# A decoder layer stack on one core: ScalarE's order in the second block of a batch, and queries transposed ahead of keys

## The reference, cut to what matters

```python
for i in range(DEPTH):                       # DEPTH = 6
    x = attn_layer(shift_tokens(x), Wqkv[i], q_scale[i], k_scale[i], Wo[i]) + x
    x = ffn_layer(shift_tokens(x), ln_g[i], ln_b[i], W1[i], b1[i], W2[i], b2[i]) + x

def attn_layer(x, Wqkv, qs, ksc, Wo):        # 16 heads of 64
    q, k, v = split(x @ Wqkv)                # per head
    q = l2norm(q) * qs; k = l2norm(k) * ksc  # then rotary tables on q and k
    out = local_attention(q, k, v)           # windows of 32, each sees itself and the one before
    return out @ Wo

def ffn_layer(x, g, bln, W1, b1, W2, b2):
    xn = (x - mu) / sqrt(var + 1e-05) * g + bln
    a, gate = split(xn @ W1 + b1, 2)
    return a * gelu(gate, exact) @ W2 + b2
```

## Time and profile before

| what | value |
|---|---|
| timed runs | 2187.67, 2188.90, 2188.56 us; median 2188.56 us |
| profiled execution, its own time | 2173.51 us |
| its span | 2171.7 us |
| PE busy | 2003.2 us, 92% |
| DVE busy | 1411.9 us, 65% |
| ACT busy | 1397.0 us, 64% |
| POOL busy | 1085.8 us, 50% |
| mean granted TensorE clock | 0.983 of full |
| chain that ended last | PE 70%, ACT 10%, issue 10%, DVE 9% |

### The profile page before, as it was taken

One profiled execution on the slowest core, in us unless ns is written; L12 is line 12 of the kernel. 1 busy time (PEld: TensorE's weight loads), 2 busy tenths in 40 slices (PEclk: granted clock), 3 DMA queues, 4 the chain that ended last, 5 costly groups with the idle time before them and its releaser, 6 DMA issues.

```text
span 2171.7 us, 74796 instructions
## 1 busy us (share of the span) xinstructions
PE 2003.2 (92%) x32616; PEld 1186.4 (55%) x32616; DVE 1411.9 (65%) x1975; ACT 1397.0 (64%) x2029; POOL 1085.8 (50%) x709
## 2 busy tenths in 40 slices
PE   8999998788999999999999999999999999999997
PEld 5655655355555555555555555555555555555552
DVE  1454444676677776767677767776777676767662
ACT  5555554466677666766676666666766676667763
POOL 0000000586666666556666656665656665666550
PEclk9999998899999999999999999999999999999998
DMA  3000000122223222232222322222322223222220
GB/s 108 2 1 1 2 20 30 37 64 61 60 70 80 75 71 62 58 94 74 72 57 68 90 55 72 73 60 66 80 76 69 62 60 90 70 70 61 61 61 20
DMA packets 82066, 128.11 MB, mean 59 GB/s; under 512 B 17230, under 2 KB 28108, under 8 KB 81740
## 3 DMA queue, kind: packets, MB, share of 16 engines
q1 hardware_dynamic: 81740, 123.33, 21.7%
HBM read 21.55 MB, written 1.05 MB: 10 GB/s over the span
## 4 chain that ended last, share of the span: by engine, by line
PE 70%; ACT 10%; issue 10%; DVE 9%; DMA 0%; ACTq 0%; DVEq 0%; SPq 0%
PE ps L617 13%; PE ps L613 12%; PE ps L639 8%; PE ps L693 6%; PE ps L678 6%; PE ps L685 5%; PE ps L426 3%; PE ps L622 3%; PE ps L626 2%; ACT work L993 2%; PE ps L658 2%; DVE work L1249 2%; DVE SS L1141 2%; PE ps L519 1%; PE ps L440 1%
## 5 line engine op out<-in xcount | busy, mean ns | idle before, releaser
L1418 POOL TENSOR_TENSOR work<-work,RS 128x1024 f32<-128x1024 f32 x192 | 365.2, 1902 | 406.4 <-ACT RS L967 405.1
L1096 DVE TENSOR_TENSOR work<-ps,work 128x512 f32<-128x512 f32 (+1 forms) x288 | 249.1, 865 | 341.1 <-ACT work L1025 304.6
L617 PEld LDWEIGHTS ps<-ident,work 128*128 128x128 f32 x3072 | 344.5, 142 | 167.9 <-issue 120.2
L617 PE MATMUL ps<-ident,work 128*128 128x128 f32 x3072 | 395.3, 276 | 25.9 <-ACT work L993 21.9
L1429 POOL TENSOR_TENSOR work<-work 128x1024 f32<-128x1024 f32 x96 | 226.9, 2364 | 124.9 <-DVE work L1101 124.8
L1437 POOL TENSOR_TENSOR work<-work 128x1024 f32<-128x1024 f32 x96 | 225.9, 2353 | 100.2 <-DVE work L1101 100.2
L1101 DVE TENSOR_TENSOR work<-ps,work 128x512 f32<-128x512 f32 (+1 forms) x288 | 247.3, 859 | 0.0
L1037 ACT ACTIVATE work<-work 128x1024 f32<-128x1024 f32 x96 | 101.5, 1057 | 206.6 <-DVE work L1181 206.3
L1141 DVE TENSOR_REDUCE SS<-work 128x16 f32<-128x1024 f32 x192 | 232.1, 1209 | 0.0
L685 PEld LDWEIGHTS ps<-work 64*32 64x32 f32 x12288 | 134.4, 105 | 148.1 <-issue 132.6
L613 PE MATMUL ps<-WQ,XS 128*128 128x512 f32 x384 | 188.6, 614 | 8.0 <-issue 4.3
(11 more groups left out here) (184 smaller groups left out, 3208.9 us busy)
## 6 DMA issues: line engine op xcount, KB each, us to landing
work<-work SPq DMA_DIRECT2D x576, 128.0 KB
work<-work SPq DMA_DIRECT2D x336, 64.0 KB
WQ<-in_wqkv SPq DMA_DIRECT2D x6, 512.0 KB, 3.7
WK<-in_wqkv SPq DMA_DIRECT2D x6, 512.0 KB, 4.5
WV<-in_wqkv SPq DMA_DIRECT2D x6, 512.0 KB, 3.5
WO<-in_wo SPq DMA_DIRECT2D x6, 512.0 KB, 3.9
work<-ZR SPq DMA_DIRECT2D x48, 64.0 KB
W<-in_w SPq DMA_DIRECT2D x6, 341.0 KB, 3.1
```

What stands on the lines that cost most here:

```text
L617: m = nc.tensor.transpose(flat(R)[:, t * 128:t * 128 + 128], src[:, t * 128:t * 128 + 128], ident[:, :])
L1096: V.tensor_tensor(h16(cos_part[:, j, cols]), h16(src), rotary_tabs[:, at:at + 64].unsqueeze(1).broadcast_to([PARTS, heads_in, 64]), ALU.mu ...
L1418: U.tensor_tensor(h16(qk_norm[:, j, :]), h16(cos_part[:, j, :]), inv_norms[:, j, :].unsqueeze(2).broadcast_to([PARTS, 16, 64]), ALU.mult). ...
```

## The change

Three moves; no instruction is added or removed.

1. In every step PE transposes the queries ahead of the keys, and ScalarE copies the transposed queries ahead of the two key halves. In the second block's step the chunk 2 pieces of the feed-forward keep their places between and behind the two.
2. In the second block's step ScalarE's first Gelu stands ahead of the values' copy, directly behind the table load.
3. `invert_norms` of the keys, at the end of the first block's step, goes into the second block's step, behind the square of the queries and the heads' copy and ahead of the table load.

```diff
@@ TensorE, step @@
                 if b:
+                    if a:
+                        pe.wait_ge(q_sin, g + 1)
+                    pe.wait_ge(q_normed, g)
+                    turn(bank_z, qk_norm[:, 0, :]).then_inc(q_turned, 1)
+                if f is not None and n == 1:
+                    pe.wait_ge(gate_gelu, 3 * f + 2)
+                    hid_gate(2, bank_f)
+                if b:
                     pe.wait_ge(k_normed, g)
                     if d:
                         pe.wait_ge(heads_turned_copied, g - 2)
                     turn(bank_y, qk_norm[:, 1, :], 0, 4).then_inc(k_turned, 1)
                     turn(bank_y, qk_norm[:, 1, :], 4, 8).then_inc(k_turned, 1)
-                if f is not None and n == 1:
-                    pe.wait_ge(gate_gelu, 3 * f + 2)
-                    hid_gate(2, bank_f)
-                if b:
-                    if a:
-                        pe.wait_ge(q_sin, g + 1)
-                    pe.wait_ge(q_normed, g)
-                    turn(bank_z, qk_norm[:, 0, :]).then_inc(q_turned, 1)
@@ ScalarE, step @@
                 if f is not None and n == 1:
+                    if b:
+                        invert_norms(g - 1, 1)
                     nc.scalar.preload_act_table_set(GELU)
+                    gelu(f, 0, bank_f)
                 if b:
...
                     A(v_rows[:, (n - 1) % 2, :], flat(bank_x), ACT.Copy).then_inc(values_copied, 1)
-                if f is not None and n == 1:
-                    gelu(f, 0, bank_f)
...
                 if b:
+                    act.wait_ge(q_turned, g)
+                    A(q_t[:, :, :], turned(bank_z), ACT.Copy).then_inc(q_turned_copied, 1)
+                if f is not None and n == 1:
+                    gelu(f, 2, bank_f)
+                if b:
                     for half in range(2):
                         act.wait_ge(k_turned, 2 * g - 1 + half)
...
-                if f is not None and n == 1:
-                    gelu(f, 2, bank_f)
-                if b:
-                    act.wait_ge(q_turned, g)
-                    A(q_t[:, :, :], turned(bank_z), ACT.Copy).then_inc(q_turned_copied, 1)
...
-                if a:
+
+                if a and not (f is not None and n == 0):
                     invert_norms(g, 1)
```

## The result

| | before | after |
|---|---|---|
| timed runs, median | 2188.11 us (2182.88 to 2188.90, 4 runs) | 2166.66 us (2163.55 to 2167.32, 4 runs) |
| profiled execution, span | 2171.7 us | 2161.7 us |
| mean granted TensorE clock | 0.983 | 0.988 |

The ratio is 0.9907 with a 95% interval of 0.9887 to 0.9927: faster by 0.9%, where I had forecast 0.3% slower and a range from 2177.

A forecast was written before the change was run, and what follows sets the result against it. TensorE, busy 2003.2 of 2171.7 us, was taken as the bound. Terms -56.0 - 11.8 + 74.9 = +7.1 us on timed 2188.6 gave 2195.7, rounded to 2195.5; range 2177 to 2208, forecast's own 2190 to 2202.

The forecast's parts named there:

- The second block's step: L622's wait on VectorE's product goes: 56.0 us gained over 23 steps, keys' projection at 9.90 in place of 12.65.
- The loss in the other steps: Keys' projection waits for the later keys' copy in third, fourth, first blocks' and five light steps: together 74.9 us lost.
- The slow clock goes with the wait: Second block's steps: clock at 0.50 behind the 2.6 us wait in seven of 23; gain seven times 1.68, 11.8 us.
- I carry that as a constant: Timed runs were 15.05 us above the profiled execution; this offset was taken as unchanged by the edit.
- rival 1: The 15 us between timed and profiled runs are nine more slow-clock stretches and go too: 2180.5; chance 0.27, wholly or in part.
- The waits at L678 stay: PE's waits for nothing shown in the score bursts, 15.0 us in 16 times, remain because their count follows the instruction stream.
- rival 2: Score bursts start later with less window traffic; half of L678's 15.0 us goes, losses come out even: 2188; chance 0.21.
- Rival 3: Clock falls in the new waits, 1.68 us each in up to 22 first block's steps: 2207 to 2232; chance 0.08.
- Rival 4: Second block's wait stays since something else holds the first product, leaving only losses: 2263, less what remains; chance 0.02.

The follow-up runs named there:

- the turns alone: Kernel before with only queries transposed and copied ahead of the keys in every step, ScalarE's Gelu and norms as before: 2248.60 us, ratio 1.0302.
- the small windows: Kernel with only the Gelu and norms moves; from the third block each value window transfer moves 64 of 512 columns, output not the reference's: 2097.25 us, ratio 0.9616.
- the queries' copy in halves: Kernel with only the Gelu and norms moves; transposed queries copied in two halves, first four score groups waiting for the first only: 2103.38 us, ratio 0.9637.
- the second profile of before: Profiled execution from running the unchanged kernel before again, no edit: 2186.12 us; the 12 executions had median 2184.12 us.
- the mask last: Whole change with the mask written into the score bank behind the key halves instead of ahead of the queries' copy: 2182.59 us, ratio 1.0001.
- the second of the pieces' kernels: Gelu and norms moves only, output projection pieces ahead of the first score burst in third and fourth blocks' steps, variance too in the first's: 2136.15 us, ratio 0.9788.
- the pieces' kernels: Gelu and norms moves only, output projection pieces ahead of the first score burst, without or with the first block's variance: 2121.52 and 2136.15 us.
- the ScalarE part: Whole change with queries and keys transposed and copied in the old order; only first Gelu and keys' norms moved: 2101.87 us, ratio 0.9630.

## Why the prediction was wrong

**The second block's step: right.** 56.0 us of wait less 2.0, step at 19.70 for 19.72. The sum took off all 56.0; the 2.0 of step g = 97 could not go.

**The loss in the other steps: right.** 74.9 us forecast; the turns alone give 64.5 net of 10.8 returned at L678 (the size 64.1), and every keys' projection stands within 0.03 us of its place.

**The slow clock goes with the wait: right in kind, wrong in size.** "I carry that as a constant", said of the 15.05 us between the profiled execution and the timed runs, is the step that failed first. They were no offset of the profiler but more slow stretches, as the mean clock and the count both show: fifteen lengths in another execution of before, where I counted seven. So the term was 25 us and not 11.8. That was rival 1; I gave it 0.27 although its size, "nine more stretches", fitted the gap. The profile of after has none in the stack between 435 and 2141. I had also read the seven as standing behind "the 2.6 us wait" each: their waits were 2.28 to 2.61 us, and the fifteen others, with 2.11 to 2.61, kept their clock.

**The waits at L678 stay: wrong.** This is the second step that failed. The sum left 15.0 us in place and rival 2 halved it; it became 1.1 (1.2 us of the 15.0 only changed their name). I named the windows' traffic as the cause. That is not what the runs show: an eighth of the bytes left 7.4 us, while the same traffic with the last copy 1.5 us ahead of the scores left 1.1 and 1.6, and 0.6 us ahead in the presence of the same waits 11.9.

**The range.** I priced rivals 1 and 2 each by itself and let the range end at 2177, just under rival 1. Both came: 2195.5 less 15 and less 7.5 is 2173 already, and less all of the 15.0 it is 2165.5.

**Rival 3, clock falling in the new waits:** it did not in the steps that I priced; the first block's step with two waits of 0.9 and 0.8 us and sixteen transposes between them runs at 1.00 throughout. But the earlier trace rows, the evidence that I held against it, was one stretch (from 456.5 to 461.5 us nothing on TensorE but transposes and waits of 0.93 and 1.21 us) that kept its 1.00. In two of the later kernels the clock fell to 0.50 in the same kind of early step, with waits of about 0.6 and 1.21 us and only transposes between the values' and the keys' projection: twice with the small windows (at 445.5 and 462.5 us), once with the queries' copy in halves (at 449.9). **Rival 4** did not happen.

Put together on medians: 2184.1 - 55.5 - 25.2 + 74.9 - 10.2 = 2168.1, measured 2166.66. Here 55.5 is the wait of the second profile of before less the 2.0 that stays, 10.2 what its waits inside the score bursts fell by (11.3 to 1.1), and 74.9 is still the forecast. The forecast's 2195.5 differs from that sum by 13.4 us of clock, 10.2 us at L678, and 4.4 us of the median of before, which three runs had shown at 2188.56.

**What the stalls are, and what stays open.** Why do the score bursts stall? The releaser column says only that PE had nothing that the profile shows to wait for. The traces say more. In all fourteen profiles 168 such waits of over 0.15 us stand inside a score burst, all of them in the second burst of their step, and all at the same place of TensorE's own instruction sequence: counted in order of start, weight loads and sequencer instructions included, at the 194th or 195th of a group of 256. The profile's instruction queue moved as many packets, each of 16384 bytes, as there are such groups; for the kernel before, 258 packets for 66127 instructions (258.3 groups):

```profile
q8 instruction: 258, 4.23, 0.8%
```

Each of the 168 waits ends 2.2 to 3.3 us after the start of such a packet. The longest in the kernel before (first block's step), and the packet in the DMA view of 1174.4 to 1174.7 us:

```profile
1175.45 0.41 PE L678 MATMUL ps<-KT,work 64*32 64x64 f32 x18
1177.25 0.70 PE L678 MATMUL ps<-KT,work 64*32 64x64 f32 x46 [1.40 <-issue]
...
q8 instruction: 1, 0.02, 25.9%
```

From these counts and times I conclude that TensorE was waiting there for its own instructions; the profile names no releaser. Ahead of these waits the packet started 0.41 to 1.45 us after the first burst's start in the kernel before (last copy 0.59 us ahead of the burst in three steps of four), 0.48 to 1.21 with the mask last (0.62), and from 0.27 before it to 0.32 after it in the whole change (1.54). A longer lead did not always go with an earlier packet: it was 0.90 us after the burst's start at a lead of 1.64 with the turns alone, and 0.77 and 0.90 at 1.60 in the second of the pieces' kernels.

The lead is not the whole of it. Taken over all of TensorE's lines of the stack, waits at that place of the sequence (194th to 196th) add up to 18.0 and 14.4 us in the two profiles of before, 10.0 in the ScalarE part, 3.3 in the whole change and 4.3 with the turns alone; the last two have both the longer lead and the new waits. With the waits but not the lead (mask last) they are 13.5, and with the lead but no waits (pieces ahead) 16.0 and 14.7, now mostly at L685. The pieces' kernels changed the order behind the scores as well, so what each of the two does by itself stays open.

## What to carry to other kernels

Three moves went in together, the two on ScalarE worth -82 us and the turns +65: time each part alone, since the sum hid a version 3% faster. When a profiled execution is faster than the timed ones, look at the mean granted clock of several executions before taking the difference for a constant: here a wait of 2.0 to 2.6 us on TensorE that recurs each period brought the clock down to 0.50 in some of its turns, in 7 of 22 in one execution of the kernel before and in 14 in another. When TensorE waits for nothing that the profile shows, count its instructions up to each such wait and look at the instruction queue. And before turning two transposes around, ask which copy the next writer of the bank waits for, and keep that one first.

## What the runs showed of the hardware that was not expected

- The same program, undisturbed, spread over 0.8% in 29 executions (2173.69 to 2191.28 us), most of it with the clock (0.981 to 0.973). The kernels without the long wait spread less or no more: 3 us in four executions of the ScalarE part, 10 us in ten with the mask last.
- A recurring TensorE wait of 2.0 to 2.6 us, with the eight transposes of the heads (1.1 us) just ahead of it, let the granted clock fall to 0.50 of full in 7, 14 and 18 of the 22 second block's steps; of 1.3 to 1.7 us once in 22; of 0.7 to 1.0 us never in these steps. Nor did two waits of 0.9 and 0.8 us around sixteen transposes in the first block's steps of the whole change. In early steps with nothing but transposes between waits of 0.6 and 1.2 us it fell three times in two kernels. In another it fell once, at 1212 us, right behind stalls of 0.37 and 1.45 us that only half a burst of weighing (31 matmuls, 0.45 us) kept apart.
- TensorE's stalls for nothing shown inside bursts of small matmuls (64 pairs in 0.8 us) came at one place in every 256 of its instructions (the 194th or 195th, 168 waits in fourteen profiles), and ended 2.2 to 3.3 us after the start of a packet of 16384 bytes on the instruction queue.
- A wait that ended with ScalarE's copy (0.11 us after its end) was shown with "issue" as its releaser.
